# Attention scores in two row tiles of 64 rows, keys held once, scores begun ahead of the output projection, and all sums of exponentials on TensorE

## The reference, cut to what matters

```python
q, k, v = proj(hs, Wq, bq, S), proj(at, Wk, bk, T), proj(at, Wv, bv, T)
scores = einsum('bhsd,bhtd->bhst', q, k) / sqrt(32)
scores = clip(scores, -50, 50)            # masked keys: -50
probs = softmax(scores); probs = probs / (probs.sum(-1) + 1e-8)
ctx = einsum('bhst,bhtd->bhsd', probs, v) # back to (8, 112, 512)
delta = layernorm(clip(rs, 0, 0.3) * (ctx @ Wo.T + bo)) * gamma + beta
x = x + delta
```

## Time and profile before

| | |
|---|---|
| time, median of 3 runs | 472.92 us (471.49 to 474.95) |
| the profiled execution | 472.69 us |
| its span | 471.0 us |
| TensorE busy | 443.2 us (94%) |
| VectorE busy | 316.1 us (67%) |
| ScalarE busy | 244.7 us (52%) |
| GpSimd busy | 111.0 us (24%) |
| the stage, from the first scores to the end of its last values | 250.3 to 352.6 us |

### The profile page before, as it was taken

The page is one execution under the profiler, slowest core; times in us unless marked ns, Lnnn a source line. Parts: engine busy times, 40 slices in busy tenths (PEclk is TensorE's granted clock), DMA queues, the critical chain, the costliest instruction groups (busy, mean ns, idle before and its releaser), DMA issues.

```text
span 471.0 us, 9958 instructions
## 1 busy us (share of the span) xinstructions
PE 443.2 (94%) x3838; PEld 279.1 (59%) x3847; DVE 316.1 (67%) x573; ACT 244.7 (52%) x370; POOL 111.0 (24%) x126
## 2 busy tenths in 40 slices
PE   8999899999899899999998888899999999999997
PEld 5556565655355345454555667577775565556996
DVE  4995596679867877765755455888867985555111
ACT  4755744764666356464847668477744682221000
POOL 2220400025024000001084364644422251000000
PEclk9999999999999999999999899899999999999999
DMA  8998988934795145333497998766242370000111
GB/s 268 328 376 310 372 292 262 330 93 146 219 295 139 53 109 160 78 91 82 111 306 197 272 316 312 266 214 225 85 135 90 90 221 26 0 0 0 48 51 58
DMA packets 59183, 82.73 MB, mean 176 GB/s; under 512 B 20100, under 2 KB 43652, under 8 KB 57988
## 3 DMA queue, kind: packets, MB, share of 16 engines
q1 hardware_dynamic: 59136, 82.14, 55.2%
q10 hardware_dynamic: 2, 0.01, 0.0%
HBM read 58.76 MB, written 14.42 MB: 155 GB/s over the span
## 4 chain that ended last, share of the span: by engine, by line
PE 68%; DVE 12%; SPq 7%; DMA 4%; issue 4%; ACT 2%; POOL 2%; ACTq 0%; DVEq 0%; POOLq 0%
PE psum L1597 13%; PE psum L208 8%; PE psum L206 8%; PE psum L1647 8%; PE psum L1430 6%; PE psum L673 4%; PE psum L1544 3%; PE psum L1439 3%; PE psum L1497 3%; DMA kst<-k_scratch 2%; SPq L237 2%; PE psum L1373 2%; PE psum L1527 2%; PE psum L1548 2%; DMA w_stage<-in_w 2%
## 5 line engine op out<-in xcount | busy, mean ns | idle before, releaser
L208 PE MATMUL psum<-wv_p,kv_p 128*128 128x512 f16 x288 | 66.1, 379 | 0.5 <-DVE khl L228 0.5
L206 PE MATMUL psum<-kv_p,wk_p 128*128 128x376 f16 x384 | 66.0, 322 | 0.3 <-DVE khl L228 0.3
L1253 ACT ACTIVATE e<-psum,mask_bias 128x448 f32<-128x448 f32 x96 | 53.6, 635 | 20.6 <-PE psum L1527 16.1
L206 PEld LDWEIGHTS psum<-kv_p,wk_p 128*128 128x128 f16 x384 | 37.5, 98 | 24.6 <-issue 0.6
L208 PEld LDWEIGHTS psum<-wv_p,kv_p 128*128 128x128 f16 x288 | 28.0, 98 | 32.8 <-issue 1.0
L1946 DVE TENSOR_SCALAR e<-e 128x1344 f32<-128x1344 f32 x32 | 32.3, 1010 | 11.5 <-ACT e L1253 11.5
L1544 PE MATMUL psum<-e,vst 128*32 128x112 f32 x768 | 34.9, 266 | 3.9 <-issue 3.3
L1597 PE MATMUL psum<-xt,wg_b 128*128 128x448 f16 x176 | 36.9, 352 | 0.3 <-issue 0.3
L1597 PE MATMUL psum<-xt,wu_b 128*128 128x448 f16 x176 | 36.9, 352 | 0.0
L1647 PE MATMUL psum<-h_p,wd_r 128*128 x176 | 36.0, 366 | 0.0
L1647 PEld LDWEIGHTS psum<-h_p,wd_r 128*128 128x128 f32 x176 | 33.1, 188 | 2.7
(11 more groups left out here) (197 smaller groups left out, 853.9 us busy)
## 6 DMA issues: line engine op xcount, KB each, us to landing
kst<-k_scratch SPq DMA_DIRECT2D x32, 384.0 KB, 6.3
kv_raw<-in_ctx_feat SPq DMA_DIRECT2D x12, 768.0 KB, 6.3
w_stage<-in_w SPq DMA_DIRECT2D x6, 1408.0 KB, 8.7
cn<-in_ctx_tok SPq DMA_DIRECT2D x8, 768.0 KB, 9.6
k_scratch<-khl SPq DMA_DIRECT2D x128, 48.0 KB, 2.0
v_scratch<-vsp SPq DMA_DIRECT2D x24, 256.0 KB, 2.8
vst<-v_scratch SPq DMA_DIRECT2D x8, 768.0 KB, 4.6
qst<-qhl SPq DMA_DIRECT2D x32, 112.0 KB, 5.2
```

The costliest lines, as they stand in the source:

```text
L206: mm = pe.matmul(psum[:, kv_bank(p), 0:TQ], wk_p[:, u, k, n * P:(n + 1) * P], src[:, v, k, 0:TQ], **ends)
L208: mm = pe.matmul(psum[:, kv_bank(p), :], src[:, u, k, n * P:(n + 1) * P], wv_p[:, v, k, :], **ends)
L1253: act.activation(e[g][:, c, :], psum[:, D_S + (TC * g + c) % 4, 0:4 * S], ACT.Exp, bias=mask_bias[:, b, c:c + 1], scale=1.0 / (WS * QS)).t ...
```

## The change

- Scores work on pairs of groups: m = 2b + pair. Two of the four heads of a group lie on partitions 0 to 63, two on 64 to 127, and the contraction has 64 rows (the high and the low half of the keys). The two halves of the queries are two matmuls that accumulate. So a chunk of a pair takes 16 matmuls, alternately on the upper and the lower 64 rows, which write two neighbouring banks. `kst` holds keys once and has four buffers (KST = 4) in the space of two; a fetch brings a pair of groups, two fetches a batch.
- `exps` takes a chunk of a pair at a time, two banks, 896 columns; `e` is two buffers of a pair. `clip` works on a chunk too, and `values` waits for each chunk.
- The first chunk of the next pair's scores is issued ahead of `project`, and the following ones around the values, both for TensorE and for the order on ScalarE and VectorE.
- `FOLDED` is empty: GpSimd sums nothing, and all sums are matmuls.

```diff
-        def keys_fetch(sp, b, g):
-            sp.dma_start(kst[b % 2][:, g].rearrange("p h t -> p (h t)"),
-                         k_scratch[b, :, :, g].rearrange("u d h (o t) -> (u d) o (h t)", o=1)
-                         .to_broadcast([2 * HD, 2, 4 * TP])).then_inc(kst_loaded[b % 2], 16)
+        def keys_fetch(sp, b, pair):
+            gs_of = slice(2 * pair, 2 * pair + 2)
+            sp.dma_start(kst[b % KST][:, gs_of].rearrange("p g j t -> p (g j t)"),
+                         k_scratch[b, :, :, :, gs_of].rearrange("r u d g j t -> (r u d) (g j t)")).then_inc(kst_loaded[b % KST], 16)
...
-        e = [at(f"e{r}", [P, TC, 4 * S], F32, 56576 + r * 5376) for r in range(4)]
+        e = [at(f"e{r}", [P, TC, 2, 4 * S], F32, 56576 + r * 10752) for r in range(2)]
-        FOLDED = [(0, 1)] * 4 + [()] * (B - 4)
+        FOLDED = [()] * B
...
@@ sync
-            for g in range(G):
-                keys_fetch(sp, 0, g)
-            sp.wait_ge(down_sum, TILES)
-            for g in range(G):
-                keys_fetch(sp, 1, g)
+            for pair in range(2):
+                keys_fetch(sp, 0, pair)
             for g in range(G):
                 sp.wait_ge(k_spilled[g], 64 * B)
             for c in range(TC):
                 sp.wait_ge(v_spilled[c], 16 * B)
+            for pair in range(2):
+                keys_fetch(sp, 1, pair)
             sp.wait_ge(wq_lo, 1)
             queries_stack(sp, 0, 0)
             queries_stack(sp, 0, 1)
             values_fetch(sp, 0, 0)
             values_fetch(sp, 1, 1)
+            sp.wait_ge(down_sum, TILES)
+            for pair in range(2):
+                keys_fetch(sp, 2, pair)
             queries_stack(sp, 1, 0)
+            for pair in range(2):
+                keys_fetch(sp, 3, pair)
             for b in range(B):
-                for g in range(G if b + 2 < B else 0):
-                    sp.wait_ge(s_sum, TC * (G * b + g + 1))
-                    keys_fetch(sp, b + 2, g)
+                for pair in range(2 if b + KST < B else 0):
+                    sp.wait_ge(s_sum, TC * (2 * b + pair + 1))
+                    keys_fetch(sp, b + KST, pair)
...
@@ scalar
-            def exps(m):
-                b, g = m // G, m % G
-                after(act, pv_sum, m - 3)
...
+            def exps(m, chunks=range(TC)):
+                b, pair = m // 2, m % 2
+                after(act, pv_sum, 2 * (m - 1))
...
+                for c in chunks:
                     act.wait_ge(s_sum, TC * m + c + 1)
-                    act.activation(e[g][:, c, :], psum[:, D_S + (TC * g + c) % 4, 0:4 * S], ACT.Exp,
+                    bank = D_S + 2 * ((TC * m + c) % 2)
+                    act.activation(e[pair][:, c], psum[:, bank:bank + 2, 0:4 * S], ACT.Exp,
                                    bias=mask_bias[:, b, c:c + 1], scale=1.0 / (WS * QS)).then_inc(e_raw, 1)
             query_hi(1, 1)
+            query_hi(1, 2)
             exps(0)
-            query_hi(1, 2)
-            exps(1)
             query_hi(1, 3)
             for b in range(B):
                 if b >= 5:
                     x3_normalized(act, b - 5)
                 if b:
                     sums_copy(b - 1)
+                exps(2 * b + 1, (0,))
                 if b >= 3:
                     context_high(act, b - 3)
                 if b >= 5:
                     turned_high(act, b - 5)
-                for g in range(G):
-                    m = G * b + g + 2
-                    if m < G * B:
-                        exps(m)
+                exps(2 * b + 1, (1, 2))
+                if b + 1 < B:
+                    exps(2 * b + 2)
@@ tensor
+            def scores(m, c):
...
+                after(pe, e_raw, TC * m + c - 1)
+                for i in range(4):
+                    g, j = 2 * pair + i // 2, i % 2
+                    for v in range(2):
+                        for r in range(2):
+                            rows = slice(64 * r, 64 * r + 64)
+                            mm = pe.matmul(psum[:, D_S + 2 * ((TC * m + c) % 2) + r, i * S:(i + 1) * S],
+                                           kst[b % KST][rows, g, j, c * P:(c + 1) * P],
+                                           qst[b // 4][rows, j, v, g, b % 4 * S:(b % 4 + 1) * S], start=v == 0, stop=v == 1)
+                mm.then_inc(s_sum, 1)
...
-            scores(0)
+            scores(0, 0)
+            scores(0, 1)
             query(1, 2)
-            scores(1)
+            scores(0, 2)
             query(1, 3)
             for b in range(B):
+                scores(2 * b + 1, 0)
                 if b >= 4:
                     project(pe, b - 4)
                     spread(b - 1)
                 if b >= 5:
                     normalized_turn(pe, b - 5)
-                for g in range(G):
-                    m = G * b + g + 2
-                    if m < G * B:
-                        scores(m)
-                    if g == 0 and 1 <= b < 4:
+                for pair in range(2):
+                    m = 2 * b + pair + 1
+                    if m < 2 * B:
+                        if pair:
+                            scores(m, 0)
+                        scores(m, 1)
+                    values(b, 2 * pair)
+                    if m < 2 * B:
+                        scores(m, 2)
+                    if pair == 0 and 1 <= b < 4:
                         spread(b - 1)
-                    if (b, g) == (B - 1, G - 1):
+                    if (b, pair) == (B - 1, 1):
                         project(pe, 4)
-                    values(b, g)
+                    values(b, 2 * pair + 1)
@@ vector
                 if b:
                     invert(b - 1)
-                if b:
-                    clip(G * b + 1)
+                clip(2 * b + 1, 0)
                 if b >= 3:
                     context_low(dve, b - 3)
                 if b:
                     normalize(b - 1)
+                clip(2 * b + 1, 1)
                 if b >= 4:
                     delta_variance(dve, b - 4)
+                clip(2 * b + 1, 2)
                 if b >= 5:
                     turned_low(dve, b - 5)
-                clip(G * b + 2)
+                clip(2 * b + 2, 0)
+                clip(2 * b + 2, 1)
                 if b >= 4:
                     x3_statistics(dve, b - 4)
-                clip(G * b + 3)
+                clip(2 * b + 2, 2)
                 if b >= 4:
                     x3_shift(dve, b - 4)
                 if b == 3:
                     dve.wait_ge(wo_hi, 1)
                     dve.scalar_tensor_tensor(wo_p[:, 1], wk_raw[:], WS, wo_p[:, 0], ALU.mult, ALU.subtract).then_inc(wo_lo, 1)
-                if b + 1 < B:
-                    clip(G * b + 4)
```

More of the change, by code:

```diff
@@ L511, in build @@
         wq_p = [at("wq_p0", [P, KC, D], F16, 79104), at("wq_p1", [P, KC, D], F16, 161344)]
-        qst = [at(f"qst{n}", [P, 4, G, HALF], F16, 94464 + n * 14336) for n in range(2)]
+        qst = [at(f"qst{n}", [P, 2, 2, G, HALF], F16, 94464 + n * 14336) for n in range(2)]
         C_BUFS = 3
@@ L559, in queries_stack, with e_head, e_group @@
                 for hh in range(4):
-                    sp.dma_start(qst[n][64 * u:64 * u + 64, hh, gs_of].rearrange("p g s -> p (g s)"),
+                    at_row = 64 * (hh // 2) + 32 * u
+                    sp.dma_start(qst[n][at_row:at_row + 32, hh % 2, :, gs_of].rearrange("p v g s -> p v (g s)"),
                                  qhl[n][32 * hh:32 * hh + 32, :, gs_of].rearrange("d v g s -> d v (g s)")).then_inc(q_stacked[n][pair], 16)
-        e = [at(f"e{r}", [P, TC, 4 * S], F32, 56576 + r * 5376) for r in range(4)]
+        e = [at(f"e{r}", [P, TC, 2, 4 * S], F32, 56576 + r * 10752) for r in range(2)]
+        def e_head(g, c, hh):
+            lo = (g % 2 * 2 + hh % 2) * S
+            return e[g // 2][:, c, hh // 2, lo:lo + S]
+        def e_group(g, c, rows):
+            return e[g // 2][0:rows, c, :, g % 2 * 2 * S:(g % 2 + 1) * 2 * S]
         rz = at("rz", [P, S], F32, 78080)
         zs = [at(f"zs{g}", [P, 4 * S], F32, where) for g, where in enumerate((194304, 194304 + 1792))]
-        FOLDED = [(0, 1)] * 4 + [()] * (B - 4)
+        FOLDED = [()] * B
         ctxt = at("ctxt", [P, KC, N], F32, 198400)
@@ L926, in down_load @@
                 sp.dma_start(wd_int[i % RING][:], wd[:, i * D:(i + 1) * D]).then_inc(wd_loaded[i % RING], 16)
-            sp.wait_ge(s_sum, TC * G * B)
+            sp.wait_ge(s_sum, TC * 2 * B)
             sp.wait_ge(pv_sum, G * (B - 1))
@@ L1243, in _ @@
             query_hi(0, 3)
-            def exps(m):
-                b, g = m // G, m % G
-                after(act, pv_sum, m - 3)
-                if b and g in FOLDED[b - 1]:
-                    act.wait_ge(z_added, 4 * (b - 1) + 2 * g + 2)
-                for c in range(TC):
+            def exps(m, chunks=range(TC)):
+                b, pair = m // 2, m % 2
+                after(act, pv_sum, 2 * (m - 1))
+                if b and pair == 0 and FOLDED[b - 1]:
+                    act.wait_ge(z_added, 4 * b)
```

(44 more changed lines are left out.)

22 lines of the change are left out of this document (13 added, 9 removed).

## The result

The kernel after takes 493.3 us (median of 4 executions, 490.2 to 495.2) where the kernel before takes 473.9 beside it: ratio 1.043 (1.038 to 1.048), slower, and above the forecast range. The profiled execution took 492.7 us (span 491.0, granted clock 0.983 on the mean, where the one before had 471.0 and 0.993). Executions that a lower clock disturbed are left out of all ratios.

What follows compares the result with a forecast made beforehand. TensorE, 68% of the chain, was taken to bound the kernel, with holes in early batches and VectorE nearly full too in late ones; -7.6 + 9.6 + 0.6 + 2.5 = +5.1 on 472.7 gave 478 us, range 466 to 489.

Steps and rivals of the forecast that it cites:

- the clock term: Whole attention stage: as many falls of the granted clock to 1.2 GHz as before, 0 us, bounds +-1.7.
- The term of +9.6: Batches 0 to 3: four of nine 256-instruction blocks arrive late under full DMA, +9.6 us, bounds 0 and 20.
- Batches 0 to 3, by TensorE's work: From the first values to the end of batch 3: TensorE's work sums to 33.4 us, where before it took 42.6.
- Start: +1.6: Start of the stage: first exponential and table load move behind the third query; first values at 260.4 instead of 258.8, +1.6 us.
- End of batch 3: +0.6: First projection waits for the output weights' low half, now behind the last clip; batch 4 13.9 against 13.3, +0.6 us.
- Batches 5 to 7: +2.5: VectorE's delta_variance stands behind a clip, so late batches lengthen and values(7, 2) wait 1.4 us; +2.5 us, bounds 0 and +5.
- B: Score matmuls on the array's two halves take turns instead of running side by side: 492 us, chance 0.10.
- A: Batches 0 to 3: instruction blocks arrive in time behind fewer key bytes, block term zero: 468 us, chance 0.27.
- C: More instruction blocks are late, six at 7.0 us, +15.5 us in all: 488 us, chance 0.13.

## Why the prediction was wrong

The step that failed most is the clock term, "as many falls: 0". The forecast's steps end at a span of 476.1 us, the measured one is 491.0. Of these 14.9 us, 7.2 are falls of the clock that no step had in it (1.7 at the start, 3.8 in batches 0 to 3, 1.7 in batch 4), 3.0 are batches 5 to 7, 1.1 TensorE's work in batches 0 to 3, 0.2 the stops, and 2.5 ahead of the stage and 0.8 behind it are not the change's.

What the change costs, by parts of the stages: 118.9 - 106.1 = 12.8 us hang on the transfers after, 102.1 - 95.3 = 6.8 before, so 6.0 are the change's; the orders are 106.1 - 97.7 = 8.4; the rest is 97.7 - 95.3 = 2.4. Sum 16.8 (the whole stage). By the ratios the same parts are 5, 9 and 6.5 us of 20, with 3 to 5 us of uncertainty in each. The rest, 2.4 or 6.5, is called TensorE's own work here, but it is what is left over and not settled closer: the changed kernel has in it a block stop of 2.53 us and 6.8 us at 1.2 GHz, the one before stops of 1.23 and 1.19 us and 3.4 us at 1.2 GHz. With the transfers present the orders came to 10.6 us, so the parts depend on the order in which they are undone.

**Bound and blocks: right.** Blocks were read rightly from the earlier trace rows. The term of +9.6 met 9.8 us of stops, though as three of 2.9 to 3.8 and not four of 2.4. By the rule of the Trainium skill ("Runtime: NRT & Kernel Launch", Instruction fetch mechanics), that crossings are mostly hidden, there would be none. The traces agree with it where the DMA share is 0.26 (270 to 290 us without fetches, no stop over 0.25 us), and not at 1.06, where the first stops of 3.10 and 3.79 us stand.

**"Batches 0 to 3, by TensorE's work", 33.4 us: too little.** Without fetches they take 35.5, busy 34.5. And the 9.2 us taken off for it were no gain of the change: without fetches the kernel before takes 35.6 for them too. The saving lay in stops, which the next term had to give back.

**"Clock: 0, +-1.7": wrong, by 7 us.** After, batches 0 to 3 have a granted clock of 0.93, and the same 1,148 matmuls are busy for 38.3 us instead of 34.5 at 1.00: 3.8 us. It fell to the level of 1.2 GHz four times in the stage for some 3.4 us each (260.6, 281.1, 301.6, 315.2 us): three times 1.2 to 1.4 us behind the end of a stop of 2.9 to 3.8 us, and once within the stop of 2.2. Before, it fell twice: at 267.9, as the stop of 2.27 ended, and at 302.1, 1.3 us behind the one of 2.29. The prediction priced stops by their length and held the number of falls fixed, though it had read itself that falls follow stops. And its sum didn't even hold them fixed: the start, 33.4 us and batch 4 are added up from durations at the upper level, but 42.6 and 13.3 us, from which they are subtracted, have the two falls of before in them (the spread at 268.5 took 2.01 us for 1.04, the projection at 301.4 took 4.45 for 2.76). "As many falls" should have been some +3.4; two falls more than before are the other half.

**"Start: +1.6": +3.3, the chain right.** The steps came in the forecast order: query, copy, table load, exponential, third chunk (behind a wait of 3.05 us), last query, two chunks. At the upper level this chain is 10.1 us from the first scores, which is the forecast; the last query and the two chunks took 4.9 us instead of 3.3 because the clock fell at 260.6. That a wait of this length stands in the chain was not said, and so no fall behind it.

**"End of batch 3: +0.6": +2.4.** The wait (2.22) was forecast at 2.3. The projection behind it was priced at 2.6 and took 4.28, mostly at half clock; a wait of two microseconds brought its own fall. Before, it had taken 4.45, behind the wait for GpSimd.

**"Batches 5 to 7: +2.5": +5.5, the mechanism half right.** The late shift was forecast at 2.5 us into the batch and the reciprocal came at 2.5; batch 7 waits for a clip, 0.53 us of the 1.4 forecast. The step that failed is which wait ends first: the prediction followed clips to `values(b, 2)` and never asked what `values(b, 0)` waits for, which is `normalize` and so the reciprocal. Batch 6 has two short stops put to issue besides (0.46, 0.35). That batch 7 took 14.9 us against 15.0 forecast is luck: its two waits (0.94 for `normalize`, 0.53 for the clip) make up for the 1.4 of one.

**Rivals.** B gave the right time, 492, by luck, from a mechanism that is false: the halves run side by side. A is refuted as a forecast, but its condition was right: without the crowded transfers the stops go. C was refuted in number, right in direction. No rival covered the case that came: several waits in series, most with a fall of the clock of their own, on steps priced without any fall. The 2.5 us ahead of the stage are scatter between executions, half as large as the forecast's whole difference.

## What to carry to other kernels

Count the instructions of the engine that leads, per microsecond, wherever the DMA queues are full: there 288 more of them cost 5.5 us without doing anything. A stop can be paid a second time, by the clock: here four of five stops of 2.2 to 3.8 us were. When a step is added up from durations at full clock, take the falls out of the time it is compared with too, or put as many in. When steps are moved in in-order engines, follow every wait of the leading engine on a bank or buffer back to its releaser, also the ones that were always over in time. When parts are undone one by one and their gains don't add, look for what takes them back.

## What the runs showed that was not expected

- Waits that are fulfilled take room in the blocks: with them, block stops in the early batches end 473 and 227 matmuls and loads apart, without them 253 to 256 or twice that. Whether each takes as much as a matmul is not shown. 288 of them cost 5.5 us, where the whole change cost 16.8.
- A block doesn't always stop TensorE in the batches with transfers: between 279.86 and 300.27 us three of four passed, at a share of 0.53 on the mean, so not under a full DMA.
- After the stop of 3.10 us that ended at 272.3 the clock didn't fall, after the 3.79 and the 2.87 us it did.
- The kernel before without its fetches is 7 us faster: that much of the stage hangs on its own transfers. No version here that computes the whole beats it.
